# A graph network's edge phase: GpSimd's index copies and loop taken out, large buffers moved to multiples of 2048 bytes

## What is computed

```python
def _sage_conv(x, src, dst, W_l, b_l, W_r):
    msgs = x[src]
    agg = jax.ops.segment_sum(msgs, dst, num_segments=N_NODES)
    deg = jax.ops.segment_sum(jnp.ones((src.shape[0],), x.dtype), dst, num_segments=N_NODES)
    mean = agg / jnp.maximum(deg, 1.0)[:, None]
    return mean @ W_l + b_l + x @ W_r
h = jax.nn.relu(_sage_conv(x, src, dst, W1_l, b1, W1_r))
h = jax.nn.relu(_sage_conv(h, src, dst, W2_l, b2, W2_r))
# x is then _layernorm(x + h @ W3 + b3)
```

## Time and profile before

| | us |
|---|---|
| median of three runs | 3079.15 |
| the profiled execution | 3074.89 |
| its span, first to last instruction | 3073.1 |
| TensorE (PE) busy | 2906.6 (95%) |
| VectorE (DVE) busy | 2441.1 (79%) |
| GpSimd (POOL) busy | 2157.1 (70%) |
| ScalarE (ACT) busy | 1991.2 (65%) |

### The profile page before, as it was taken

How to read it: one execution, slowest core, us unless ns; L and a number is a source line. 1 busy time by engine, 2 the same in 40 slices (tenths; PEclk the granted TensorE clock), 3 DMA queues, 4 the chain that set the end, 5 groups by cost and what they waited for, 6 DMA issues and landing times. The chain is left out here.

```text
span 3073.1 us, 56079 instructions
## 1 busy us (share of the span) xinstructions
PE 2906.6 (95%) x18457; PEld 2594.6 (84%) x18457; DVE 2441.1 (79%) x4001; ACT 1991.2 (65%) x2992; POOL 2157.1 (70%) x1830
## 2 busy tenths in 40 slices
PE   5999999999999999999999999999999898888885
PEld 4888888888888888888888888888888787777774
DVE  5888787878878788787887878778787797777775
ACT  4677676766767677676766767677676555454554
POOL 5777777767777677776767767676676467776766
PEclk9999999999999999999999999999999899999998
DMA  3444444444444444444444444444444465555553
GB/s 129 145 164 149 139 162 151 154 148 149 156 151 151 143 164 149 139 161 151 155 147 149 156 151 151 143 164 149 140 162 145 157 225 194 195 200 197 201 195 125
DMA packets 253118, 488.22 MB, mean 159 GB/s; under 512 B 37616, under 2 KB 165207, under 8 KB 253091
## 3 DMA queue, kind: packets, MB, share of 16 engines
q1 hardware_dynamic: 202498, 387.58, 37.2%
q0 software_dynamic: 50176, 99.91, 10.5%
q10 hardware_dynamic: 416, 0.40, 0.0%
HBM read 284.67 MB, written 206.22 MB: 160 GB/s over the span
## 5 line engine op out<-in xcount | busy, mean ns | idle before, releaser
L496 ACT ACTIVATE h_full<-pair,bias 128x512 f32<-128x512 f32 x784 | 532.1, 686 | 716.5 <-PE pair L870 696.4
L658 DVE TENSOR_TENSOR h_lo<-h_full,h_hi 128x1024 fp32r<-128x1024 f32 x392 | 645.8, 1647 | 196.8 <-ACT h_hi L498 171.0
L393 POOL TENSOR_TENSOR xb<-xn,b_row 128x1024 f32<-128x1024 f32 x196 | 470.5, 2401 | 312.5 <-DVE y L680 310.6
L347 POOL DMA_INDIRECT xe<-in_x_dram,e_stage x392 | 501.8, 1280 | 176.9 <-issue 97.4
L881 PE MATMUL pair<-w_hi,h_hi 128*128 128x256 f32 x1960 | 563.6, 288 | 20.9 <-DVE h_lo L658 19.0
L881 PE MATMUL pair<-w_hi,h_lo 128*128 128x256 f32 x1960 | 554.2, 283 | 0.0
L881 PE MATMUL pair<-w_lo,h_hi 128*128 128x256 f32 x1960 | 551.0, 281 | 0.0
L498 ACT CAST h_hi<-h_full 128x1024 fp32r<-128x1024 f32 x392 | 412.4, 1052 | 12.5
L870 PE MATMUL pair<-xt_hi,w_hi 128*128 128x512 f32 x980 | 406.0, 414 | 6.4 <-DVE xt_lo L654 4.3
L509 ACT ACTIVATE o<-y,nb,rs 128x256 f32<-128x256 f32 x784 | 407.0, 591 | 5.8 <-DVE nb L711 5.2
L881 PEld LDWEIGHTS pair<-w_hi,h_hi 128*128 128x128 f32 x1960 | 369.1, 188 | 41.6 <-DVE h_lo L658 31.5
(11 more groups left out here) (126 smaller groups left out, 6429.6 us busy)
## 6 DMA issues: line engine op xcount, KB each, us to landing
xn<-in_x_dram SPq DMA_DIRECT2D x196, 512.0 KB, 3.5
out_dram<-o SPq DMA_DIRECT2D x196, 512.0 KB
seg<-seg_tab SPq DMA_DIRECT2D x74, 512.0 KB
xdb_tab<-xdb SPq DMA_DIRECT2D x49, 512.0 KB
h_tab<-src_h SPq DMA_DIRECT2D x49, 512.0 KB
h_tab<-dst_h SPq DMA_DIRECT2D x49, 512.0 KB
xn<-h_tab SPq DMA_DIRECT2D x49, 512.0 KB
xb<-xdb_tab SPq DMA_DIRECT2D x49, 512.0 KB
```

What stands on the lines that cost most here:

```text
L347: nc.gpsimd.indirect_dma_start(out=xe[:, kind, s], out_offset=None, in_=x, in_offset=bass.IndirectOffsetOnAxis(ap=e_stage[:, kind, s:s + 1 ...
L393: nc.gpsimd.tensor_tensor(xb[:, b], xn[:, u], b3_row[:, :].unsqueeze(1).to_broadcast([P, S, D]), ALU.add).then_inc(xb_ok, 1)
L496: nc.scalar.activation(h_full[:, n, k], ps[:, k], ACT.Relu, bias=bias[:, n, k:k + 1]).then_inc(hf_ok[n], 1)
L658: nc.vector.tensor_tensor(h_lo[:, h], h_full[:, n], h_hi[:, h].bitcast(f32), ALU.subtract).then_inc(hlo_ok[n], 1)
```

## The change

GpSimd's edge phase is written out for all 49 steps, the index columns are read where they lie in `h_row` and `idx`, and `c_stage`, its copies, their waits and the counting register go. The other engines keep their loops. The SBUF buffers are declared in another order: a pad of 1920 bytes, then the large buffers, whose sizes are multiples of 2048 bytes, then the small ones.

```diff
-        ident = sb("ident", [P, P])
+        pad = sb("pad", [P, 480])
         w_raw = sb("w_raw", [P, 5, K, D])
...
-        bias = sb("bias", [P, 2, K])
-        b1_row = sb("b1_row", [P, D])
-        b3_row = sb("b3_row", [P, D])
...
-        stats = sb("stats", [P, S, 6])
-        mv = sb("mv", [P, 2, S, 2])
...
+        ident = sb("ident", [P, P])
+        bias = sb("bias", [P, 2, K])
...
-        c_stage = sb("c_stage", [P, 2, 2, S], i32)
...
             def fetch(j, b):
                 after(pool, c_hs_in[b], 0 if isinstance(j, int) and j < 2 else slot_use(j - 2, b, 16 * S))
                 after(pool, c_hs_ps, (j - 1) * K)
-                nc.gpsimd.tensor_copy(c_stage[:, b, 0], h_row[:, bass.ds(j * S, S)]).then_inc(stage_ok, 1)
-                wait_staged()
                 for s in range(S):
                     nc.gpsimd.indirect_dma_start(
                         out=xn[:, b, s], out_offset=None, in_=h_tab,
-                        in_offset=bass.IndirectOffsetOnAxis(ap=c_stage[:, b, 0, s:s + 1], axis=0)).then_inc(c_hs_in[b], 16)
+                        in_offset=bass.IndirectOffsetOnAxis(ap=h_row[:, j * S + s:j * S + s + 1], axis=0)).then_inc(c_hs_in[b], 16)
 
             def scatter(j, b):
                 after(pool, c_out[b], 0 if isinstance(j, int) and j < 2 else slot_use(j - 2, b, 16 * S))
-                nc.gpsimd.tensor_copy(c_stage[:, b, 1], idx[:, 2, bass.ds(j * S, S)]).then_inc(stage_ok, 1)
-                wait_staged()
-                pool.wait_ge(c_o_ok, pool.snap(scattered, min_val=1, max_val=NE))
-                pool.reg_add(scattered, scattered, 1)
+                pool.wait_ge(c_o_ok, j + 1)
                 for s in range(S):
                     nc.gpsimd.indirect_dma_start(
-                        out=out, out_offset=bass.IndirectOffsetOnAxis(ap=c_stage[:, b, 1, s:s + 1], axis=0),
+                        out=out, out_offset=bass.IndirectOffsetOnAxis(ap=idx[:, 2, j * S + s:j * S + s + 1], axis=0),
                         in_=o[:, b, s], in_offset=None, bounds_check=N - 1, oob_is_err=False).then_inc(c_out[b], 16)
 
-            scattered = pool.alloc_register("scattered")
-            pool.reg_mov(scattered, 1)
...
-            edge_passes(pool, step)
+            for j in range(NE):
+                step(j, j % 2, min(NE - 1 - j, 2))
             pool.wait_ge(stage_ok, pool.snap(staged) - 1)
-            pool.wait_ge(c_o_ok, pool.snap(scattered) - 1)
```

More of the change, by code:

```diff
@@ L81, in build @@
         o = sb("o", [P, 2, S, D])
-        stats = sb("stats", [P, S, 6])
-        mv = sb("mv", [P, 2, S, 2])
-        sd = sb("sd", [P, 2, S])
-        rs = sb("rs", [P, 2, S])
-        nb = sb("nb", [P, 2, S])
         xe = sb("xe", [P, 2, S, D])
@@ L98, in build @@
         xdb = sb("xdb", [P, S, D])
+        ident = sb("ident", [P, P])
+        bias = sb("bias", [P, 2, K])
+        b1_row = sb("b1_row", [P, D])
+        b3_row = sb("b3_row", [P, D])
+        b1_hi = sb("b1_hi", [P, K, 2], f32r)
+        b1_lo = sb("b1_lo", [P, K, 2], f32r)
+        bias_c = sb("bias_c", [P, K])
+        eps = sb("eps", [P, 1])
+        stats = sb("stats", [P, S, 6])
+        mv = sb("mv", [P, 2, S, 2])
+        sd = sb("sd", [P, 2, S])
+        rs = sb("rs", [P, 2, S])
+        nb = sb("nb", [P, 2, S])
         idx = sb("idx", [P, 3, NT], i32)
```

## The result

| | before | after |
|---|---|---|
| median of four runs, us | 3078.53 | 2992.8 |
| lowest to highest | 3075.53 to 3080.98 | 2990.8 to 2994.8 |
| the profiled execution, its span | 3074.89, 3073.1 | 2990.85, 2989.1 |
| mean clock granted to TensorE | 0.988 | 0.992 |

The ratio is 0.9722 (0.9707 to 0.9737): 2.8% faster. In a later batch of runs, on chip 15, the same changed kernel gave only 0.9925 (0.9907 to 0.9944); that is the last part of the experiments.

The account below looks back on a forecast made before the run. GpSimd was taken to bound the edge phase: 13.01 - 0.48 - 1.26 + 0.10 = 11.37 us a step. Steps 68.9, head 1.6 and tail 6.2 sum to 76.7 us saved, giving 2998.2 profiled or 3002.4 median; range 2962 to 3031.

Parts of the forecast that it names:

- The bound: Edge phase: GpSimd's own program sets the step of 13.01 us and stays the bound at 11.37, over a floor of 10.24.
- The copies: GpSimd, edge phase: the busy time of a step's two index copies goes, 0.48 us a step.
- The waits behind them: GpSimd, edge phase: idle between copy and transfer goes, 1.26 us a step, with some 6 us of long gaps staying.
- the end of the bound that was taken: Idle ahead of each group of four transfers: bounds 0.30 and 0.85 to 1.04 us, 0.30 taken.
- Stretching: Edge phase: transfers lengthened under VectorE operations with two SBUF inputs; 0.84 us a step remains and 0.10 is added.
- Head and steps: Edge phase: 42 steps save 1.64 us each, 68.9 us; earlier starts of fetches 2 and 6 save 1.6 together.
- Tail: From GpSimd's copy for fetch 48 to the last scatter's end: 51.0 us shortens by 6.2, the computing path being late next.
- The loop written out: GpSimd's longer straight-line program in the edge phase: put at 0; stalls, if any, priced at 10 us.
- The layout: Node phase: moved buffers put at 0; bounds were all of an 8% excess in matmul spacing gone, 190 us, or as much added.
- tenth of the 8%: Rival, node phase faster: a tenth to all of the matmul spacing's 8% excess goes, 2983 down to 2812 us; chance 0.08.
- the sign that was named for the layout: Start of the edge phase, 2413 before: a shift by more than 3 us would be the layout's doing.
- The rival of a new bound: Edge phase: TensorE or VectorE becomes the bound if stretching vanishes, GpSimd needing 10.3 us a step, 2958 in all; chance 0.12.

Follow-up runs that it names:

- e4: The changed kernel with VectorE's three edge-phase operations that read both inputs from SBUF replaced by reductions over one SBUF input; 2950.22 us, ratio 0.9584.
- e5: The changed kernel with `xe_lo` and `y` reading SBUF in place of PSUM, so five operations a step have two SBUF inputs; 3049.29 us, ratio 0.99.
- e8: The changed kernel with h and the mean kept in PSUM, leaving one operation a step with two SBUF inputs; 3064.22 us, ratio 0.9953.
- e9: The changed kernel with scan, mean and h in place in PSUM, leaving no edge-phase VectorE operation with two SBUF inputs; 3062.96 us, ratio 0.9954.
- e2: The new order of the buffers with the old GpSimd program, so the changed kernel without its program change; 3064.83 us, ratio 0.9956.
- e3: The changed kernel, steps written out, with both copies to `c_stage` and the waits behind them put back; 3061.52 us, ratio 0.9949.
- e10: The changed kernel run again with no edit, on chip 15; 3055.2 us, ratio 0.9925.
- e13: The changed kernel with the two copies and their waits kept for batches 0 to 25 alone, on chip 2; 3050.89 us, ratio 0.9913.
- e1: The new GpSimd program with the old order of the buffers, so the changed kernel without its layout; 3006.26 us, ratio 0.9757.
- e6: The changed kernel with a pad 64 bytes longer, so all large buffers start 64 past a multiple of 2048; 3056.51 us, ratio 0.9927.

## Why the prediction was right, step by step

- **The bound.** GpSimd, and with it the whole edge phase, as read from the earlier trace rows. Forecast 11.37 us a step, measured 11.337.
- **The copies.** Gone, 0.48.
- **The waits behind them.** Forecast 1.26. The idle went from 158.1/41 = 3.86 a step to 8 x 0.305 = 2.44: 1.42. The 6 us of long gaps as in the earlier trace rows that were to stay went with the copies: after has no gap of GpSimd over 0.32 from 2480.5 to 2930. Nothing stands in front of a group of four, the end of the bound that was taken.
- **Stretching.** Forecast +0.10; fetches went from 1.059 to 1.100 and scatters from 1.112 to 1.127, 4 x 0.041 + 4 x 0.015 = 0.22. Mis-sized by 0.12, and it cancels most of the 0.16 by which the line above was off: that 11.37 lies so near 11.337 is in part luck. That two-input instructions cause it was argued from four rows; e4, e5, e8 and e9 show it. The second theory drawn from the Trainium skill's page "SBUF — State Buffer", section "Who interferes with whom", that `tensor_tensor` stalls no such transfer, is not borne out: 1.97 us at 2756.76 in the trace, and fetches of 1.100 us on average against 0.962 in e4. The first, that a VectorE instruction with two SBUF inputs contends, is.
- **Head and steps.** 68.9 + 1.6 = 70.5 forecast, 75.2 less the tail's 4.4 = 70.8 measured.
- **Tail.** From GpSimd's first work on fetch 48 to the end 51.0 us before, 44.8 forecast, 46.6 measured: 4.4 saved, not 6.2. After still waits 2.30 and 1.16 us for `o` (2959.25 and 2965.63), and the twelve scatters behind the second wait take 12 x 1.29 us without a hole, where the forecast had one group of four left. (The forecast's 3053.4 for the last `o` cannot be read from the earlier trace rows, which give 3052.91, when ScalarE became free; VectorE's `nb` ended at 3053.31.)
- **The loop written out.** Forecast 0, measured 0 within noise (e2 against e3).
- **The layout.** Forecast 0; measured 8.8 us in the node phase, the step of the working that failed. Inside a group of twelve, matmuls of 512 columns start 0.228 us apart instead of 0.234 (the groups that begin with `xt_hi`, 500 to 600 us), those of 256 still 0.12. The argument was that operands at 800 and at 640 show a like excess. But `xt_lo` began 32 past a multiple of 64 and `w_hi` on one; the first moved, the second did not, and the excess of 512-column matmuls only fell from 0.021 to 0.015 us. The spacing is not the whole account: over 500 to 2000 us the 88 such starts inside groups save 0.41 us a pass, and about half of it is lost again, most of that where TensorE goes from transposes to the next matmul (0.148 us before, 0.184 after). The "tenth of the 8%" of the rival (2983, 19 us) was over twice too much, and its sign was right. The start of the edge phase moved by 8.8 us, the sign that was named for the layout.

The sum was thus 76.7 forecast against 84.0 of span; of the 7.3 between them the layout is 8.8, the tail -1.8 and the steps and the head 0.3; the range held the result. What no row of before could tell is that the gain hangs on the chip or the time of the run. On chips 13 and 15 the changed kernel, or its copy moved by 64 bytes, gave 0.7% in place of 2.8: the floor that was read as 10.24 us a step from one trace is near 12.6 there. The 3055.2 of e10 lies outside the forecast's range (2962 to 3031), so that the comparison met no gaps is luck. The rival of a new bound had the right mechanism (TensorE takes over) and the wrong number, because it took TensorE's pace for a constant.

## What to carry to other kernels

Where a queue's own timeline shows it never waiting for others, count its idle pieces: a copy of 0.2 us that a transfer has to wait for left 0.85 to 1.04 us of idle time in place of 0.30, and in all cost four times its own length (1.59 us for two). Keep indices where the transfer can read them. Know which VectorE instructions read two operands from SBUF while GpSimd issues transfers; three of them cost about one microsecond in eleven. Reading one operand from PSUM frees the transfers, but in e8 and e9 TensorE then waited for the PSUM buffers, and no run here shows it as a gain. And measure a gain that pushes another engine towards its floor on more than one chip before it is believed: the old kernel's medians were the same on every chip (3075 to 3079), and by e13 that is because it never asked for the faster pace.

## What the runs showed of the hardware that was not expected

- An indirect DMA of GpSimd that starts inside a `tensor_tensor` of 1.22 us with two SBUF inputs ends 2.03 to 2.12 us after that instruction began, wherever in it the transfer started (84 of 84 in after), so it takes up to 2.09 us instead of 0.95 to 1.03. One that starts just ahead of it, or within its first 0.02 us, is untouched (0.94 to 0.95 for eleven such fetches), and then `mean` itself takes 1.26 to 1.28 us instead of 1.22.
- The 4096-byte packets of the last scatters, with no gather beside them, took 178 ns in before and 176 in e1, and 159 in after and e2 (medians): the layout's doing. With the buffers at 64 past a multiple of 2048 (e6) it was 179, though TensorE's gain was there in full. Those of the gathers ahead of the first scatter took 164 in before and 159 in e1, after, e2 and e6. The Trainium skill, "DMA: Bandwidth & Descriptors", section "How a descriptor splits into AXI transactions", says that a descriptor that does not start on a multiple of 256 bytes fetches bytes that it does not use; the scatters, which fetch from the moved buffer `o`, agree with it. So the layout has two effects with two conditions. In e1 transfers average 1.141 and 1.179 us, in after 1.100 and 1.127; whether the packets do that was not tried by itself.
- TensorE can start its instructions about 0.7 us apart for some 10 us, with nothing to wait for that the profile shows, in some batches of runs and not in others, and with the same kernel.
